# One part of a fused block on one core: output projection with channels on partitions, gated by ScalarE and turned back on TensorE

## The reference, cut to what matters

```
mod = (_silu(L0_c) @ L0_wmod).reshape(L0_c.shape[0], 6, 1, -1)
sa, ca, ga, sb, cb, gb = ...
ga = (2 * (ga >= 0) - 1) * jnp.maximum(jnp.abs(ga), 0.25)
h = _layernorm(x, axis=-1) * (1 + ca) + sa
# in _L0_attn_ref(h, ...):
    y = (y + D_param * xb) * jax.nn.silu(z)
    return residual + y @ W_out          # residual is h
x = x + ga * _L0_attn_ref(h, ...)
h = _layernorm(x, axis=-1) * (1 + cb) + sb
x = x + gb * _L0_ffn_ref(h, ...)
```

## Time and profile before

| | |
|---|---|
| median of 3 runs | 2683.87 us (2680.85 to 2685.65) |
| the profiled execution's own time | 2684.5 us |
| its span | 2682.7 us |
| mean granted clock of TensorE | 0.953 of full speed |
| busy, PE / DVE / ACT / POOL | 88% / 89% / 54% / 83% of the span |
| DMA | 541.96 MB, mean 202 GB/s |

### The profile page before, as it was taken

How to read it: one execution, slowest core, us unless ns; L and a number is a source line. 1 busy time by engine, 2 the same in 40 slices (tenths; PEclk the granted TensorE clock), 3 DMA queues, 4 the chain that set the end, 5 groups by cost and what they waited for, 6 DMA issues and landing times.

```text
span 2682.7 us, 28375 instructions
## 1 busy us (share of the span) xinstructions
PE 2356.5 (88%) x9006; PEld 1678.2 (63%) x9006; DVE 2389.6 (89%) x2390; ACT 1453.2 (54%) x2765; POOL 2229.8 (83%) x1559
## 2 busy tenths in 40 slices
PE   6356998979899898998989899898989989798899
PEld 2224675756667676666757666676666667566678
DVE  4998999999998999999999999999999999999822
ACT  5656556465555656565565655556564664654220
POOL 2888989888898898889889898989889898987812
PEclk9678999999999999999999999998999999999899
DMA  5997988979798897979889897988979798797911
GB/s 156 241 224 184 225 197 217 224 191 239 189 220 200 207 227 190 246 178 225 208 207 228 186 245 184 218 210 198 234 187 235 185 228 216 188 237 171 233 52 49
DMA packets 308279, 541.96 MB, mean 202 GB/s; under 512 B 46352, under 2 KB 156944, under 8 KB 308128
## 3 DMA queue, kind: packets, MB, share of 16 engines
q0 software_dynamic: 72960, 243.30, 47.9%
q1 hardware_dynamic: 235168, 296.84, 35.4%
HBM read 295.10 MB, written 10.06 MB: 114 GB/s over the span
## 4 chain that ended last, share of the span: by engine, by line
PE 52%; POOL 16%; DVE 13%; issue 8%; ACT 7%; DMA 4%; SPq 0%; POOLq 0%; DVEq 0%; ACTq 0%
PE wbank L508 19%; PE mbank L520 10%; PE wbank L409 7%; DVE hbank L766 7%; POOL unit L1354 6%; PE wbank L450 4%; PE wbank L537 4%; POOL gsum L1366 2%; DMA gsum<-unit 2%; ACT z L940 2%; POOL act L1321 2%; POOL stat L1242 2%; PE wbank L534 2%; PE wbank L420 2%; PE wbank L470 1%
## 5 line engine op out<-in xcount | busy, mean ns | idle before, releaser
L1354 POOL TENSOR_TENSOR unit<-dtx,b_bc 128x1024 f32<-128x1024 f32 x512 | 1384.1, 2716 | 40.2 <-DVE dtx L843 29.3
L766 DVE TENSOR_TENSOR_SCAN hbank<-hbank,unit 128x1024 f32<-128x1024 f32 x512 | 1173.3, 2292 | 63.0 <-ACT hbank L1127 58.7
L1127 ACT ACTIVATE hbank<-dt,a_neg 128x512 f32<-128x512 f32 x1024 | 668.8, 681 | 213.5 <-DVE unit L779 207.5
L779 DVE TENSOR_TENSOR unit<-hbank,c_bc 128x1024 f32<-128x1024 f32 x448 | 546.4, 1220 | 20.7
L1366 POOL DMA_DIRECT2D gsum<-unit x448 | 502.0, 1121 | 62.8 <-DMA gsum<-unit 30.7
L1321 POOL TENSOR_TENSOR act<-act,w_all 128x512 f32<-128x512 f32 x256 | 386.3, 1509 | 199.4 <-DVE act L744 183.9
L520 PE MATMUL mbank<-down_t,act 128*128 128x256 f32 x2048 | 524.1, 393 | 27.5 <-POOL act L1321 26.0
L508 PE MATMUL wbank<-h_t,up_t 128*128 128x256 f32 x2048 | 505.7, 391 | 36.2 <-DVE xb L637 27.2
L508 PE MATMUL wbank<-h_t,gate_t 128*128 128x256 f32 x2048 | 488.4, 381 | 8.9 <-DVE xb L637 7.8
L520 PEld LDWEIGHTS mbank<-down_t,act 128*128 128x128 f32 x2048 | 398.2, 197 | 134.8 <-POOL act L1321 46.6
L508 PEld LDWEIGHTS wbank<-h_t,up_t 128*128 128x128 f32 x2048 | 394.9, 195 | 138.8 <-DVE xb L637 38.8
(11 more groups left out here) (142 smaller groups left out, 2310.1 us busy)
## 6 DMA issues: line engine op xcount, KB each, us to landing
gsum<-unit POOLq DMA_DIRECT2D x448, 512.0 KB, 7.5
b_bc<-bc_scratch SPq DMA_DIRECT2D x352, 256.0 KB, 6.8
c_bc<-bc_scratch SPq DMA_DIRECT2D x352, 256.0 KB, 6.4
w_all<-w_scratch SPq DMA_DIRECT2D x256, 256.0 KB, 4.4
ht<-in_L_attn_x_dram SPq DMA_DIRECT2D x16, 512.0 KB, 4.0
w_out<-in_L_attn_W_out_dram SPq DMA_DIRECT2D x16, 512.0 KB, 6.6
ht<-in_L_attn_x_dram POOLq DMA_DIRECT2D x16, 512.0 KB, 7.7
out_dram<-xt SPq DMA_DIRECT2D x16, 512.0 KB, 3.3
```

The costliest lines, as they stand in the source:

```text
L766: eng.tensor_tensor_scan(h, h, unit[:, g % RING, :, :].rearrange("p a t -> p (a t)"), 0.0, ALU.mult, ALU.add).then_inc(scanned, 1)
L779: eng.tensor_tensor(o, hbank[g % HB][:, :, :], c_bc[:, s:s + 1, :].to_broadcast([P, 2, T]), ALU.mult).then_inc(c_scaled, 1)
L1127: eng.activation(hbank[g % HB][:, a, :], dt[:, 2 * q + a, :], ACT.Exp, scale=a_neg[:, 2 * q + a, n:n + 1]).then_inc(decayed, 1)
L1354: eng.tensor_tensor(unit[:, g % RING, :, :], dtx[:, 2 * q:2 * q + 2, :], b_bc[:, s:s + 1, :].to_broadcast([P, 2, T]), ALU.mult).then_inc(d ...
```

## The change

W_out is loaded once and stays as it is. The projection is made with channels on partitions: for each of the two blocks of 128 channels a bank gets four products with W_out as the stationary and `gz` as the moving operand (512 columns), and four products of 128 columns that turn `ht` and add it. ACT copies each of these banks to `gated` (the buffer `z2`) with the gate as a factor for each partition. Then PE makes the old two banks with tokens on partitions: the identity times x, which SP has loaded into `xt`, and two 128-column products that turn `gated` back. ACT's copy to `xt` with the sums stays. POOL's two multiplications and its adding DMA are gone, and so is the load of W_out for each row; the gate is loaded as a column (256 values) rather than a broadcast row, and x by a plain load of SP.

```diff
@@ streams
-            plan += [("step_sizes1", slot, 9, 1, 8), ("load_wo", slot, 1, 38, 40), ("load_ga", slot, 1, 33, 48), ("scale_wo", slot, 1, 40, 50),
-                     ("scale_h", slot, 2, 57, 61), ("gates", slot, 9, 34, 42),
+            plan += [("step_sizes1", slot, 9, 1, 8), ("load_ga", slot, 1, 33, 48), ("load_res", slot, 1, 50, 55),
+                     ("gates", slot, 9, 34, 42),
@@ TensorE
             def project(row):
-                for h in range(2):
-                    t = fill(("proj", row, h))
+                for f in range(HK):
+                    t = fill(("gated", row, f))
                     y = work.at["y", row, DK - 1]
                     need.wait_ge(y.free, y.after)
-                    need.wait_ge(wo_made, row + 1)
+                    need.wait_ge(wo_in, 16)
+                    part = slice(f * P, (f + 1) * P)
+                    for k in range(DK):
+                        eng.matmul(t.bank[:, :], w_out[:, k, part], gz[:, k, :], start=k == 0, stop=False)
+                    for q in range(TT):
+                        m = eng.matmul(t.bank[:, q * P:(q + 1) * P], ht[:, row % 2, q, part], ident[:, :], start=False,
+                                       stop=q == TT - 1)
+                    m.then_inc(t.full, 1)
+                    yield
+                for h in range(2):
+                    g = work.at["gated", row, HK - 1]
+                    t = fill(("proj", row, h))
+                    need.wait_ge(g.free, g.after)
                     need.wait_ge(res_in, 16 * (row + 1))
                     for u in range(TT // 2):
-                        for k in range(DK):
-                            c = (h * TT // 2 + u) * P
-                            m = eng.matmul(t.bank[:, u * H:(u + 1) * H], gz[:, k, c:c + P], w_out[:, k, :],
-                                           start=k == 0, stop=False)
-                        m = eng.matmul(t.bank[:, u * H:(u + 1) * H], ident[:, :], ht[:, row % 2, h * TT // 2 + u, :],
-                                       start=False, stop=True)
+                        q = h * TT // 2 + u
+                        eng.matmul(t.bank[:, u * H:(u + 1) * H], ident[:, :], xt[:, row % 2, q, :], start=True, stop=False)
+                        for f in range(HK):
+                            m = eng.matmul(t.bank[:, u * H + f * P:u * H + (f + 1) * P], gated[:, f, q * P:(q + 1) * P],
+                                           ident[:, :], start=False, stop=f == HK - 1)
                     m.then_inc(t.full, 1)
-                    yield
                     yield
@@ ScalarE
             def project(row):
 
+                xb_ready(need, min(row + 1, NB - 1))
+                for f in range(HK):
+                    t = work.at["gated", row, f]
+                    need.wait_ge(t.full, t.after)
+                    need.wait_ge(ga_in, 16 * (row + 1))
+                    eng.activation(gated[:, f, :], t.bank[:, :], ACT.Copy, scale=ga_col[:, f:f + 1]).then_inc(t.free, 1)
+                    yield
                 for h in range(2):
...
-                    yield
                     yield
@@ GpSimd
-            def scale_wo(row):
...
-            def scale_h(row):
...
@@ SyncE
-            def load_wo(row):
...
+            def load_res(row):
+                if row >= 2:
+                    need.wait_ge(row_out, 16 * (row - 1))
+                else:
+                    t = work.at["turned", max(n for n in range(len(chunks)) if n % 3 == row), 1]
                     need.wait_ge(t.full, t.after)
-                eng.dma_start(w_out[:, :, :], d["L0_attn_W_out"].rearrange("(k p) n -> p k n", p=P)).then_inc(wo_in, 16)
+                eng.dma_start(xt[:, row % 2, :, :], d["L0_attn_x"][row].rearrange("(t p) h -> p t h", p=P)).then_inc(
+                    res_in, 16)
+                if row == 0:
+                    eng.dma_start(w_out[:, :, :], d["L0_attn_W_out"].rearrange("(k p) n -> p k n", p=P)).then_inc(wo_in, 16)
                 yield
 
             def load_ga(row):
                 if row:
-                    need.wait_ge(wo_made, row)
-                    need.wait_ge(h_scaled, row)
-                eng.dma_start(ga_row[:, :], mod_dram[row:row + 1, 2 * H:3 * H].to_broadcast([P, H])).then_inc(ga_in, 16)
+                    t = work.at["gated", row - 1, HK - 1]
+                    need.wait_ge(t.free, t.after)
+                eng.dma_start(ga_col[:, :], mod_dram[row:row + 1, 2 * H:3 * H].rearrange(
+                    "b (q p) -> p (b q)", p=P)).then_inc(ga_in, 16)
                 yield
```

More of the change, by code:

```diff
@@ L149, in build @@
         xn_t = sb("xn_t", [P, HK, T])
-        ga_row = sb("ga_row", [P, H])
+        ga_col = sb("ga_col", [P, HK])
         gb_row = sb("gb_row", [P, H])
@@ L165, in build @@
         mod_row = conv[:, 1, :].rearrange("p (a h) -> p a h", h=H)
+        gated = conv
         act = sb("act", [P, MOE_RING, 2, HT])
@@ L207, in build @@
         mod_first, h_first, z_first = sem("mod_first"), sem("h_first"), sem("z_first")
[L208 to L209 removed]
+        x_in, res_in, mods_in, wo_in = sem("x_in"), sem("res_in"), sem("mods_in"), sem("wo_in")
         ga_in, gb_in, cols_in = sem("ga_in"), sem("gb_in"), sem("cols_in")
@@ L1029, in gates @@
                     if row:
-                        p = work.at["proj", row - 1, 1]
+                        p = work.at["gated", row - 1, HK - 1]
                         need.wait_ge(p.full, p.after)
@@ L1041, in project @@
                     if row >= 2:
-                        need.wait_ge(row_out, 16 * (row - 1))
                         need.wait_ge(rnorm_p, 4 * (row - 1))
@@ L1383, in _ @@
             stage_of = {"norms": norms, "step_sizes0": lambda r: step_sizes(r, 0),
-                        "step_sizes1": lambda r: step_sizes(r, 1), "stats": stats, "scale_wo": scale_wo,
-                        "scale_h": scale_h}
+                        "step_sizes1": lambda r: step_sizes(r, 1), "stats": stats}
             first_norm()
@@ L1419, in load_x @@
                 if row >= 2:
-                    t = work.at["proj", row - 2, 1]
+                    t = work.at["gated", row - 2, HK - 1]
                     need.wait_ge(t.full, t.after)
@@ L1430, in load_x @@
                 yield
-            def load_wo(row):
-                if row:
-                    t = work.at["proj", row - 1, 1]
+            def load_res(row):
[3 more added lines that the diff above has]
+                    t = work.at["turned", max(n for n in range(len(chunks)) if n % 3 == row), 1]
                     need.wait_ge(t.full, t.after)
-                eng.dma_start(w_out[:, :, :], d["L0_attn_W_out"].rearrange("(k p) n -> p k n", p=P)).then_inc(wo_in, 16)
+                eng.dma_start(xt[:, row % 2, :, :], d["L0_attn_x"][row].rearrange("(t p) h -> p t h", p=P)).then_inc(
+                    res_in, 16)
+                if row == 0:
+                    eng.dma_start(w_out[:, :, :], d["L0_attn_W_out"].rearrange("(k p) n -> p k n", p=P)).then_inc(wo_in, 16)
                 yield
@@ L1563, in _ @@
             need.wait_ge(mod_out, 16)
-            stage_of = {"load_x": load_x, "load_wo": load_wo, "load_ga": load_ga, "load_gb": load_gb, "rows_bc": rows_bc,
+            stage_of = {"load_x": load_x, "load_res": load_res, "load_ga": load_ga, "load_gb": load_gb, "rows_bc": rows_bc,
                         "weigh": weigh, "chunks": lambda r: turning}
```

## The result

The changed kernel takes **2763.44 us** (median of 4 runs, 2762.66 to 2764.46), the kernel before beside it 2684.18 us: ratio 1.0297, 95% interval 1.0279 to 1.0315, or +79.3 us. Forecast were 2745 us (+61) in a range from 2714 to 2768. The span of its profile is 2760.9 us, 78.2 more than before; the mean granted clock is 0.944 (before 0.953).

The account below looks back on a forecast made before the run. Each slot was taken as a PE stage of some 94 us, then some 63 us set by small steps and DVE. Slots 65, tail 4, less POOL's 4 and the last slot's 4, gave +61 us: 2745 us, range 2714 to 2768.

Parts of the forecast that it names:

- PE's work: In each row's projection, PE's passes grow from 8.66 to 12.14 us, +3.5 us a row.
- The place of the last bank: Last token bank filled at the fourth yield, not the third: two down products ahead of it put 0.86 us on the path.
- PE pays more: Rival, 16%: longer idling before the turn slows logits, up to 18 us (2763 us); a less hidden weight load, up to 40.
- Row 0's projection: Before the first logits: its later last bank counted with +4.0 us.
- POOL's relief: Two multiplications and a DMA issue go, about 5.5 us a row; credited 0.3 us a row and 4 us in the last slot.
- ACT, DMA and SP at nothing: Gated copies on ACT, at 1.5 us a row, and the changed loads are hidden, so they add no time.
- DVE unchanged: DVE's busy time stays the same in the profile after, with no gain from less contention with POOL.

Follow-up runs that it names:

- place alone: Kernel before with each projection bank filled one yield later on PE and ACT, no work added: 2711.97 us, ratio 1.0105.
- the wait filled: Changed kernel with two overwritten products of 512 columns ahead of the turn, where PE had waited: 2742.01 us, ratio 1.0215.
- the place mended: Changed kernel with its projection spread over moments 15 to 21 rather than 15 to 23: 2736.14 us, ratio 1.0194.
- PE's work alone: Kernel before with the passes of the two token banks made first and overwritten, POOL's work as before: 2738.07 us, ratio 1.0198.

## Why the prediction was right, and where it was short

- **PE's work, +3.5 us a row:** right. PE is busy for all of the 89.50 us from 1114.00 to 1203.50 us, up to the end of the next projection, as forecast. The added passes alone cost 3.76 us a slot, the passes of 128 columns took 0.111 us, and the last bank ended 17.36 us after the start. The weight load's 190 ns were hidden.
- **The place of the last bank, +0.86 us:** right in itself (logits start 4.4 us later, for 4.3), but **this is the term that was mis-sized.** It was priced at the time moved, and the slow logits were made a rival with 16% on the ground of the earlier trace rows, read as logits behind which PE had waited. The fast ones have the same waits, so these rows couldn't say what a longer wait would do. The move brings the wait from 1.47 to 2.30 us, and with it half the clock at the logits of every slot. Three pairs measure that part: +1.28 us a slot (place alone against before), 1.25 (changed kernel against the one with the wait filled, a direct measure, as the place is the same), and 2.19 - 0.86 = 1.33 (against the one with the place mended). Over 14 slots it is 18 us, and the place cost 2.14 us a slot, not 0.86.
- **PE pays more, 2763 us:** this rival is what happened. Its 11 x 1.65 = 18 us fit the sum, in part by luck: at the logits themselves the changed kernel pays 14 x 1.08 = 15 us (means of 3.53 and 2.45 us). The rest lies elsewhere; the clock stays at half in the products behind them, until 1060 us at row 5.
- **Row 0's projection:** counted with 4 us, it cost none. The start is 1.5 us shorter; PE waited 13.21 us for the norm before that turn and now 8.55, so the work fell into a wait. The kernel with PE's work alone has 8.48 us there and starts 3.1 us earlier than the kernel before. (The start varies from 230.73 to 235.20 us among all profiles here, so the 1.5 us may be chance.) This error of 5.5 us goes against the first, by luck.
- **POOL's relief, 0.3 us a row and 4 us in the last slot:** by itself it gave 0.00 us a slot and 5.9 in the last interval; in the changed kernel that interval is 1.0 us shorter although it holds the last projection's 4 us, so some 5 us. With a spread of over 3 us between kernels that have POOL's steps, the 4 us are neither confirmed nor refuted.
- **ACT, DMA and SP at nothing:** not contradicted, within the 0.20 us a slot in which the place mended and the added work alone differ. **DVE unchanged:** its scans take 2291 ns in the median, as in the earlier trace rows; DVE waits 63.6 us for decays in the whole run, 58.7 before.
- **The rest:** forecast and measured differ by 14 x 1.75 = 24.5 us in the slots: 1.3 a slot for the clock, 0.26 for PE's 3.76 in place of 3.5, 0.1 for POOL (0.3 credited, 0.2 for POOL, ACT and DMA together), 0.1 unexplained. Only the first of these is well above what the profiles resolve. Less 5.5 at the start and 1.0 in the last slot this gives the 18 us between +61 and +79.

## What to carry to other kernels

Price a move on the chain twice: the time that it moves, and what a longer wait does to the clock of the products behind it. Here 0.86 us of lost cover cost 2.14 us a slot, and where every row had the slow products, dummy work in the wait, or a projection spread over two moments less, gave more back than the 0.86 (1.25 and 2.19 us a slot). An engine that is 83% busy but not on the chain returned nothing in the slots for 6 us less work a row, so follow the chain first; and when a step is moved in a fixed order, look at what it now stands ahead of on each engine, since twice the bank or the norm came earlier and the wait came back elsewhere.

## What the runs showed of the hardware

The clock at the logits is not set by the wait alone: with the same waits of 1.46 to 1.50 us, the logits of the kernel before take 1.93, 1.93, 2.14, 2.27, 2.37 and 3.46 us in six rows that follow each other, and begin again at 1.93. A wait of 2.3 us ahead of the turn gives 3.56 or 3.57 us in 26 of 28 rows of two kernels with different work (3.09 and 3.12 in the others). The granted clock of such stretches, for logits of 1.93, 2.14 and 3.45 us of the kernel before (columns as in the earlier trace rows):

```profile
1024.20:1025.90 1.70, 1.68 (x16) 1.70 (x16) 1.70 (x1) 0.00 (x0) 1.70 (x3) 1.00 0.71 246
1338.70:1340.80 2.10, 2.08 (x17) 2.10 (x17) 2.06 (x2) 0.00 (x0) 2.10 (x3) 0.88 0.64 206
865.70:869.10 3.40, 3.40 (x17) 3.40 (x17) 3.01 (x2) 0.00 (x0) 3.40 (x3) 0.52 0.86 181
```

So 1.93 us is the time at the full 2.4 GHz (1.00) and the 3.57 us of the changed kernel the time at 1.2 GHz (0.50); a stretch with 0.88 has part of its time at each level. What makes the drift from row to row wasn't tried.

The Trainium skill (TensorE: Matmul & The Clock Gate, HAM oscillation — how this bites in real kernels) describes a loop in which the waits between groups of products throttle each next group anew. The changed kernel agrees, here with waits for ScalarE: the clock is 1.00 before the turn, 0.50 at the logits and 1.00 again before the next slot's turn; a wait that grew by 0.8 us cost 18 us of 2763 that way.
